# Cross-attention scores paired on the two row halves of TensorE, with scratch laid out for 4 KB reads

## What is computed

```python
# x, ctx: 8 x 256 x 512, float32; 32 query heads of 16 in 8 groups, each group with one key and value head
def layer(x):
    x = x + tanh(g_xattn) * xattn(layernorm(x), ctx, ctx)
    x = x + tanh(g_ffn) * ffn(layernorm(x))
def xattn(q, k, v):
    qh = (q @ Wq.T) -> (8, 32, 256, 16);  kh, vh = (k @ Wk.T), (v @ Wv.T) -> (8, 8, 256, 16), each repeated 4 times
    attn = softmax(qh @ kh.T / sqrt(16))
    return (attn @ vh) @ Wfc.T + bfc
def ffn(h):
    comb = sum(softmax(top_2(h @ router.T)))
    return mlp(h, shared 2048) + mlp(h, routed 256) * comb      # mlp: silu(h @ g.T) * (h @ u.T) @ d.T
```

## Time and profile before

| | us |
|---|---|
| Three runs: median (lowest, highest) | 951.03 (944.7, 956.66) |
| The profiled execution | 942.72 |
| Its span, first to last instruction | 940.9 |
| TensorE busy, granted clock over the span | 899.5, 0.987 of full speed |
| VectorE, ScalarE, GpSimd busy | 646.6, 343.4, 486.7 |

### The profile page before, as it was taken

The page is one execution under the profiler, slowest core; times in us unless marked ns, Lnnn a source line. Parts: engine busy times, 40 slices in busy tenths (PEclk is TensorE's granted clock), DMA queues, the critical chain, the costliest instruction groups (busy, mean ns, idle before and its releaser), DMA issues.

```text
span 940.9 us, 14873 instructions
## 1 busy us (share of the span) xinstructions
PE 899.5 (96%) x4896; PEld 697.8 (74%) x4896; DVE 646.6 (69%) x1083; ACT 343.4 (37%) x637; POOL 486.7 (52%) x485
## 2 busy tenths in 40 slices
PE   4689999999999999999999999999999999999998
PEld 3556766676677665688888888887688888888887
DVE  6678888778878887566656566567766656566566
ACT  5165566556655686212212122136212211122112
POOL 4201201300130299878766696663778766696650
PEclk9789999999999999999999999999999999999999
DMA  8863344435343420211111121111312111121102
GB/s 277 201 144 80 78 116 74 108 80 118 62 96 83 87 37 25 90 45 67 45 60 52 45 67 45 45 57 56 112 45 68 45 54 57 45 67 45 45 1 89
DMA packets 42346, 70.83 MB, mean 75 GB/s; under 512 B 5312, under 2 KB 21184, under 8 KB 42048
## 3 DMA queue, kind: packets, MB, share of 16 engines
q1 hardware_dynamic: 42304, 70.29, 27.9%
HBM read 55.33 MB, written 14.68 MB: 74 GB/s over the span
## 4 chain that ended last, share of the span: by engine, by line
PE 72%; issue 17%; DVE 4%; DMA 3%; POOL 2%; ACT 2%; SPq 0%; POOLq 0%; DVEq 0%; ACTq 0%
PE bank L1241 21%; PE bank L1243 20%; PE bank L1242 20%; PE bank L1316 3%; PE bank L1296 3%; PE bank L1306 3%; PE bank L1246 1%; POOL xa L461 1%; DMA q_scr<-qx_l 1%; POOL cx_l L430 1%; DVE mcol L887 1%; PE bank L1565 1%; DVE x_l L1206 1%; DMA wfc_raw<-wfc 1%; DMA xa<-x 1%
## 5 line engine op out<-in xcount | busy, mean ns | idle before, releaser
L887 DVE TENSOR_REDUCE mcol<-bank 128x2 f32<-128x512 f32 x256 | 169.8, 677 | 48.9 <-PE bank L1296 48.1
L1241 PE MATMUL bank<-x_l,w_h 128*128 128x512 f32 x504 | 197.5, 392 | 2.7 <-DVE u L1077 2.5
L1243 PE MATMUL bank<-x_h,w_h 128*128 128x512 f32 x504 | 196.4, 390 | 0.0
L1242 PE MATMUL bank<-x_h,w_l 128*128 128x512 f32 x504 | 196.4, 390 | 0.0
L740 ACT ACTIVATE probs<-bank 128x512 f32<-128x512 f32 x256 | 150.1, 594 | 120.6 <-PE bank L1306 119.5
L595 ACT ACTIVATE hT_h<-bank 128x512 fp32r<-128x512 f32 x72 | 43.2, 599 | 360.3 <-DVE bank L1179 351.5
L551 POOL TENSOR_TENSOR w_l<-raw,w_h 128x512 fp32r<-128x512 f32 (+1 forms) x144 | 162.1, 1159 | 2.9
L1089 DVE SCALAR_TENSOR_TENSOR xa<-bank,tgf,xa 128x512 f32<-128x512 f32 x128 | 96.1, 751 | 77.7 <-PE bank L1243 77.6
L1296 PE MATMUL bank<-k_st,q_st 65*128 65x256 f32 x512 | 114.0, 312 | 11.8 <-DMA q_st<-q_scr 7.1
L1296 PEld LDWEIGHTS bank<-k_st,q_st 65*128 65x128 f32 x512 | 92.9, 201 | 43.1 <-DVE mcol L887 16.6
L430 POOL TENSOR_TENSOR cx_l<-cx_raw,cx_h 128x512 fp32r<-128x512 f32 x12 | 15.5, 1295 | 191.4 <-ACT cx_h L595 191.4
(11 more groups left out here) (148 smaller groups left out, 1362.8 us busy)
## 6 DMA issues: line engine op xcount, KB each, us to landing
raw<-w_gu SPq DMA_DIRECT2D x36, 512.0 KB, 3.3
q_st<-q_scr SPq DMA_DIRECT2D x96, 128.0 KB, 3.8
dnraw<-w_dn SPq DMA_DIRECT2D x36, 256.0 KB, 2.6
xa<-x SPq DMA_DIRECT2D x4, 1024.0 KB, 7.6
cx_raw<-ctxT SPq DMA_DIRECT2D x16, 256.0 KB, 3.4
q_scr<-qx_h SPq DMA_DIRECT2D x16, 256.0 KB, 2.1
q_scr<-qx_l SPq DMA_DIRECT2D x16, 256.0 KB, 2.2
out<-xa SPq DMA_DIRECT2D x16, 256.0 KB, 2.0
```

The lines of the kernel that those rows point to most:

```text
L887: v.tensor_reduce(mcol[:, par, at:at + 2], bank[u % sm_banks(n)][:, :].rearrange("p (r k) -> p r k", r=2), AX.X, ALU.max).then_inc(max_ok, 1)
L1241: mm(out, a_h, b_l, start=start, stop=False, skip_group_check=onto)
L1242: mm(out, a_l, b_h, start=False, stop=False, skip_group_check=onto)
L1243: return mm(out, a_h, b_h, start=False, stop=stop, skip_group_check=onto)
```

## The change

Queries, keys and matmuls are arranged anew for two groups of heads at once.

- **Row halves.** The first group of a chunk has rows 0 to 47, the second rows 64 to 111 (`ROWS` = 64, `SM` = 48 rows for maximum scores, row 48 of each half for the maxima, `ST` = 49). `sm_pair` and `st_pair` issue the two groups' matmuls in turn, on tiles of 64 x 128 of the array, each into a bank of its own. The zero rows are gone, and the memset that made them.
- **Banks.** Maximum scores go round banks 0, 1 and 5. The transposed maxima move from bank 5 to bank 4 (shared with the values, so `mt_job` waits for `ob_ok`, and the value matmuls wait for `mt_cp`). TensorE's order is written by pairs `v` = 0 to 3, with the side work at new places: key and value projections in steps 2 and 3, queries in steps 4 to 7, the output projection of batch 0 in steps 6 and 7.
- **Scratch.** `q_scr` and `k_scr` have the batch outside, and the weights' rows are reordered on the host so that a dimension's four heads lie together: 4 KB a row. A read of queries is now four DMAs, for each half one of 32 rows (source: 2 parts x 16 rows) and one of 16 rows; so is a read of keys. A write has two pieces of 1 KB a row.
- **SyncE.** A `q_st` slot is free when the step's value matmuls are done (`pv_ok`, by `scored`), not its scores (`st_full`). `write_q` of chunk 0, 1, 2 now stands at the end of steps 4, 5, 6 (before: 3, 5 and 6, 6), context loads ahead of `put_max`.
- **Split results** have one place per batch (`aT_h0`, `aT_h1`, and the low parts), `aT` has two; the last batch needs no detour by `qx_h`.

```diff
-CONSTS = 2
-SM = P // 2 + 1
+CONSTS = 1
+SM = 3 * DH
 MROW = SM
 ST = MROW + 1
+ROWS = P // 2
...
-    q_scr = nc.dram_tensor("q_scr", (2, BLOCKS, CHUNKS, P, BLOCK), f32, kind="Internal").ap()
-    k_scr = nc.dram_tensor("k_scr", (2, BLOCKS, P, BLOCK), f32, kind="Internal").ap()
+    q_scr = nc.dram_tensor("q_scr", (2, BLOCKS, CHUNKS, 2, P, S), f32, kind="Internal").ap()
+    k_scr = nc.dram_tensor("k_scr", (2, BLOCKS, 2, P, S), f32, kind="Internal").ap()
...
+        def sm_bank(n, s, u):
+
+            return bank[u % 4] if isinstance(n, int) and n < 2 else bank[(0, 1, 5)[(UNITS * s + u) % 3]]
...
+            def scored(n):
+
+                sp.wait_ge(pv_ok, 4 * n)
...
-                for row, part in ((0, 0), (DH, 0), (2 * DH, 1)):
-                    src = q_scr[part, tb, c, :, bb * S:(bb + 1) * S].rearrange("(h d) q -> d h q", d=DH)
-                    sp.dma_start(r(q_st[row:row + DH, c, :, :]), src).then_inc(q_rd[c], 16)
+            def write_q(tb, oc):
+                for part, (done, tile) in enumerate(((q_hi, qx_h), (q_lo, qx_l))):
+                    sp.wait_ge(done, CHUNKS * tb + oc + 1)
+                    sp.dma_start(q_scr[part, tb, oc, :, :, :].rearrange("b p q -> p b q"),
+                                 r(tile[:, oc % 2, :]).rearrange("p (b q) -> p b q", q=S)).then_inc(q_wr[oc], 16)
...
+            def read_q(tb, bb, c, n, fresh):
+
+                if not fresh:
+                    scored(n)
+                sp.wait_ge(q_wr[c], 32 * (tb + 1))
+                for e in range(2):
+                    at, rows = e * ROWS, slice(e * ROWS, (e + 1) * ROWS)
+                    sp.dma_start(r(q_st[at:at + 2 * DH, c, :, :]).rearrange("p h q -> p (h q)"),
+                                 q_scr[0:2, tb, c, bb, rows, :].rearrange("a (d h) q -> a d (h q)", d=DH)).then_inc(q_rd[c], 16)
+                    sp.dma_start(r(q_st[at + 2 * DH:at + 3 * DH, c, :, :]).rearrange("d h q -> d (h q)"),
+                                 q_scr[0, tb, c, bb, rows, :].rearrange("(d h) q -> d (h q)", d=DH)).then_inc(q_rd[c], 16)
...
+                for e in range(2):
+                    at, rows = e * ROWS, slice(e * ROWS, (e + 1) * ROWS)
+                    sp.dma_start(r(k_st[at:at + DH, bb, :, :]).rearrange("d c q -> d (c q)"),
+                                 k_scr[0, tb, bb, rows, :].rearrange("(d c) q -> d (c q)", d=DH)).then_inc(k_rd[bb], 16)
+                    sp.dma_start(r(k_st[at + DH:at + 3 * DH, bb, :, :]).rearrange("p c q -> p (c q)"),
+                                 k_scr[0:2, tb, bb, rows, :].rearrange("a (d c) q -> a d (c q)", d=DH)).then_inc(k_rd[bb], 16)
...
+                    if s == 4 and not last:
+                        read_k(t + 1, 0)
+                    if s >= 4 and not last:
+                        write_q(t + 1, s - 4)
...
-                        if not last and s in (3, 6) and u == 0:
-                            q_low(nx, s // 6)
...
+                        if (s, u) in ((4, 7), (5, 5), (6, 5), (7, 5)):
                             q_low(nx, s - 4)
...
+                    pe.wait_ge(max_ok, UNITS * n + 2 * v - (0 if s == 0 and v == 0 else 1))
                 for j in range(2):
...
+                    for e in range(2):
+                        rows = slice(e * ROWS, e * ROWS + SM)
+                        last = mm(sm_bank(n, s, 2 * v + e)[:, j * S:(j + 1) * S],
+                                  q_st[rows, c, 2 * half + j, qt * P:(qt + 1) * P], k_st[rows, bb, c, :],
+                                  start=True, stop=True)
+                        if j == 1:
+                            last.then_inc(sm_full[e], 1)
...
+                    pe.wait_ge(exp_ok, UNITS * n + 2 * v)
+                for e in range(2):
+                    rows = slice(e * ROWS, e * ROWS + ST)
+                    mm(STB[e][:, :], k_st[rows, bb, c, kt * P:(kt + 1) * P], q_st[rows, c, 2 * half:2 * half + 2, :],
+                       start=True, stop=True).then_inc(st_full[e], 1)
```

More of the change, by code:

```diff
@@ L108, in build @@
         att.close()
-        def a_split(high, last_batch):
-            if last_batch:
-                part = qx_h if high else qx_l
-                return part[:, :, :].rearrange("p a (b q) -> p (a b) q", q=S)
-            return aT_h if high else aT_l
+        a_split = {True: (aT_h0, aT_h1), False: (aT_l0, aT_l1)}
         pflat = probs[:, :, :, :].rearrange("p a r s -> p (a r s)")
@@ L338, in body @@
                     n = STEPS * t + s
-                    if s + 3 < STEPS or not last and s != 6:
+                    if s + 3 < STEPS or not last:
                         e = s + 3
@@ L541, in split_gu @@
             def split_gu(G, f):
-                if isinstance(G, int) and G < 2:
-                    pool.wait_ge(st_full, UNITS * (N - 2) if G == 0 else UNITS * N)
-                else:
+                if is_at(G, 1):
+                    pool.wait_ge(st_full[0], UNITS // 2 * N)
+                    pool.wait_ge(st_full[1], UNITS // 2 * N)
+                if not (isinstance(G, int) and G < 2):
                     pool.wait_ge(full[3], G - 1)
@@ new lines, in body @@
+                        if not first:
+                            if s in (1, 2) and u == 3:
+                                f_sum(t - 1, 1, s - 1)
+                            if s == 1 and u == 7:
+                                f_stats(t - 1, 0, 1)
+                            if s == 2 and u == 6:
+                                f_stats(t - 1, 1, 0)
+                            if s == 3 and u == 4:
+                                f_stats(t - 1, 1, 1)
+                        if last:
+                            if (s, u) in ((5, 3), (6, 1)):
+                                f_sum(t, 0, s - 5)
+                            if (s, u) in ((6, 4), (7, 4)):
+                                f_stats(t, 0, s - 6)
+                            if s == 0 and u == 0:
+                                dve.wait_ge(ln2_stats, HTILES)
+                                for i in range(HTILES):
+                                    aggregate(1, i, ln2_var)
+                            if s == 0 and u == 5:
+                                norm2_rows(0, 0, HTILES)
+                            continue
@@ L1286, in f_part @@
                     last.then_inc(f_mm, 1)
-            def sm_unit(n, u, bb, c):
-                qt, g2, half = u // 2 % 2, u // 4, u % 2
-                banks = sm_banks(n)
-                if not (isinstance(n, int) and n == 0 and u < banks):
-                    pe.wait_ge(max_ok, UNITS * n + u + 1 - banks)
-                for j in range(2):
-                    h = g2 * RH + half * 2 + j
-                    last = mm(bank[u % banks][:, j * S:(j + 1) * S], q_st[0:SM, c, h, qt * P:(qt + 1) * P],
-                              k_st[0:SM, bb, 2 * c + g2, :], start=True, stop=True)
-                last.then_inc(sm_full, 1)
@@ new lines, in st_pair @@
+            def st_pair(n, v, bb, c):
+                kt, half = v // 2, v % 2
+                if isinstance(n, int) and n == 0 and v == 0:
+                    pe.wait_ge(max_ok, 2 * UNITS)
+                else:
+                    pe.wait_ge(exp_ok, UNITS * n + 2 * v)
+                for e in range(2):
+                    rows = slice(e * ROWS, e * ROWS + ST)
+                    mm(STB[e][:, :], k_st[rows, bb, c, kt * P:(kt + 1) * P], q_st[rows, c, 2 * half:2 * half + 2, :],
+                       start=True, stop=True).then_inc(st_full[e], 1)
@@ L1476, in body @@
-                        if s == 7 and u == 5 and not last:
-                            pe.wait_ge(q_lo, CHUNKS * nx + 3)
+                                pe.wait_ge(f_add, TILES * t - 2)
+                            x_job(nx, 0)
+                        if s == 0 and v == 3:
+                            pe.wait_ge(x_lo, TILES * nx + 1)
+                            x_job(nx, 1)
+                        if s == 1 and v in (1, 3):
+                            pe.wait_ge(x_lo, TILES * nx + 2 + v // 2)
+                            x_job(nx, 2 + v // 2)
@@ new lines, in body @@
+                        if s == 2 and v == 0:
+                            pe.wait_ge(x_lo, TILES * nx + 4)
+                            vt_job(t, 1)
+                        if s == 2 and v == 1:
+                            pe.wait_ge(vt_cp, 2 * t + 2)
+                            kv_part(nx, 0, 0)
+                        if s == 2 and v == 2:
+                            if not first:
+                                pe.wait_ge(f_add, TILES * t)
+                            kv_part(nx, 1, 0)
```

527 lines of the change are left out of this document (251 added, 276 removed).

## The result

| | before | after |
|---|---|---|
| Median, us (lowest, highest) | 953.85 (944.7, 958.81), 4 runs | 1032.17 (1024.39, 1037.6), 4 runs |
| Ratio, 95% interval | | 1.0827 (1.0714 to 1.0939) |
| Profiled execution, us | 942.72 | 1037.6 |

The forecast was 980 us with a range up to 998: the direction was right, the size was not. On the profiled execution's scale it was 972 against 1037.6, 66 us too low.

A forecast was written before the change was run, and what follows sets the result against it. TensorE bounded the kernel before, VectorE close behind; after, late reads on two engines would. Three blocks 22, last block 3 and start 4.6 add 29.6 us to 942.7: 972, 980 on the median's scale; range 912 to 998, the forecast's own 962 to 998.

The forecast's parts named there:

- The two engines: Query and key reads: each 32-row DMA with a 2-part source runs on two DMA engines, inferred from small-packet counts.
- The step as a chain of read, scores, values, next issue: Attention step: the next read is issued after the values and its landing gates the next scores; at least 9.85 us.
- Step 5's write behind the key read: Step 5's query read needs a write queued behind the key read: 7 us more a block.
- The pairs' 1.88 us: Attention scores on TensorE: two paired matmuls cost one, saving 1.88 us a step at best.
- the 0.5 for cuts: TensorE in attention: five more changes of the array's cut add 0.5 us a step.
- The feed-forward part: After attention: every matmul there is unchanged, so it should stay at 550 us.
- rival (a): Attention: reads on all 16 engines, pairs overlap, steps of 9.5 us; 31 us less, 920; chance 0.30.
- Rival (c): Attention: reads on 16 engines, pairs run one after another, cut changes add 16 us, 967; chance 0.08.
- 4.6 more: Kernel start: slower first reads delay the first transposed scores from 51.23 to 55.8 us.
- 3 x 92.0 = 276: First three attention blocks: each takes 92.0 us against 84.8, 7.2 more, 22 in all.
- 136 / 16 x 0.7 = 5.95 us, landed 7.85 us after the first issue.: A step's reads on two engines: 5.95 us of transfer plus 1.9 fixed, against 3.8 us landing before.
- 2.0 us into the step.: When a step's read is issued: after 0.5 us of score pairs, 1.0 of values, 0.5 for end and wake-up.

The follow-up runs named there:

- e1_wide: Changed kernel with only its read patterns re-cut to an outermost count of 16, for sixteen DMA engines: 914.23 us, ratio 0.9606 to the kernel before.
- e2_scored: Changed kernel, reads left on two engines; SyncE waits ahead of a read for the previous step's transposed scores, not its values: 989.38 us, ratio 1.0402.
- e3_order: Changed kernel, reads left on two engines; in step 4 the first query chunk's write goes ahead of the key read: 1014.32 us, ratio 1.0645.
- e4_same: e1_wide with both groups' score matmuls on the first group's rows, so a pair shares one row half: 971.22 us, ratio 1.0209 to the kernel before.
- e11_again: The changed kernel itself, unaltered, measured again beside e10_rows on the same chip: 1026.54 us, ratio 1.0758 to the kernel before.
- e10_rows: Changed kernel with unused 128-row matmuls ahead of the waits of steps 1 (10) and 6 (26), except the first block's step 1: 1020.53 us, ratio 1.0683.
- e9_fill: Changed kernel with unused 48-row matmuls ahead of the long waits, 10 in step 1 and 26 in step 6: 1025.53 us, ratio 1.0757.

## Why the prediction failed in size

**Right.** The two engines, from the census. The step as a chain of read, scores, values, next issue: e1_wide breaks it at the landing, e2_scored at the issue, and both shorten it. Step 5's write behind the key read (e3_order). The pairs' 1.88 us, and roughly the 0.5 for cuts (e4_same: 1.88, and 0.2 to 0.4). In the 1.88 there was luck: the value matmuls are on column strips, not on row halves, and they stand twice as dense as the maximum scores (1.00 / 16 = 0.06 us against 0.12), not four times as I had read. The feed-forward part. And rival (a), "the reads run on all 16 engines and the pairs overlap", 31 us less: e1_wide made it true, and its profiled execution is 29.1 us under that of before (942.72 - 913.62), with steps of 9.35 us where I had 9.5 (by the medians it is 39 us, 914 against 953). Rival (c), 967, is e4_same's 971.

**Wrong.** By the same cuts, the 66 us that I missed lie in three places. The second key read of the first block went out at 76.87 us instead of 57.76, 19.1 later where the forecast had "4.6 more": 14.5. The three blocks took 318.2 us where the forecast had 3 x 92.0 = 276: 42.2. And from 395.03 us to the end it is 640.7 us against 628.7 from 312.18, 12 more where the forecast had 3: 9. The steps that failed:

- *"136 / 16 x 0.7 = 5.95 us, landed 7.85 us after the first issue."* Reads with nothing ahead of them landed after 8.6 to 8.8 us (141.61 to 150.22 and 243.65 to 252.49 in e11_again, 251.95 to 260.65 in after). The 0.7 us came from two medians whose difference is small, so an error of 15% was hidden in it: 136 KB / (8.7 - 1.9) us is 20 KB a us, not 22.9. The plain steps bear it out: 2.0 + 8.7 = 10.7, and from the read of step 6 to those of step 7 and of the next step 0 it is 10.8 and 10.7 (263.80, 274.57, 285.24). That is 0.85 us in each of 24 steps of the three blocks, 20 us.
- *"2.0 us into the step."* The 0.5 for pairs and 1.0 for values hold at full clock only. After the 7.5 us wait the next read went out 3.1 us behind the first score. That a wait lowers the clock of the work behind it had no term in my sum at all, and this is the error of kind, not of size. TensorE's busy time is 85.4 us a block against 73.0 in e1_wide with the same instructions, 12 us of stretched work; of it e10_rows shows 1.7 us on the path behind one of the waits. With 20 us for the landing, 22 of the blocks' 42 are left, 7 a block, for the clock behind all waits and for what I have not found. By SyncE's read issues 12.7 of them lie in steps 0 to 2, which share their engines with context loads and a key read (43.1, 40.2 and 40.1 us, where 3 x 10.7 + 2.8 + 2.0 = 36.9 would be the forecast with the landing put right), and 6.9 in steps 4 and 5 (31.6, 32.2 and 32.5 against 29.8), of which e10_rows takes 4.0 off. How much of the 12.7 is clock and how much queueing no run tells.
- *"27.25 + 1.9 + 4 x 5.95 + 2.8 = 55.8: 4.6 more"*, the start. The first transposed scores, to which this figure is compared, began at 65.49 us, 14.3 after those of before (51.23), and the first steps add the other 4.8 of the 19.1. In e1_wide the second key read goes out at 62.45, 4.7 later than before, though its first scores wait for their read for 4.9 us only (6.0 before); the two engines add 14.4. I had counted the transfers but not SyncE's own waits. The second query read could not be issued until its write, itself queued behind the first key read, had landed: 34.94 to 40.05 in the timeline of SyncE. The third chunk's write stands behind it in SyncE's order and went out at 42.31 (37.82 in e1_wide), and the first scores wait 13.0 us.

The range failed for the same reason. Its upper end, 998, took in a key read that hides nowhere, not a mechanism by which one lateness makes the next: read late, clock low, next issue later.

## What to carry to other kernels

Read the access pattern of a DMA from its outermost dimension: here a source with 2 outermost was carried by two engines, though its rows were 4 KB, and putting the dimension of 16 outside took a step's reads from 8.7 to 4.6 us and the kernel from 1032 to 914. Making scratch rows longer does not make up for it. When a transfer turns from hidden to late, count everything that follows: who issues the next one, behind which work, and at what clock that work runs after a wait.

## What the hardware showed that I had not expected

- What two engines cost the others' transfers. Context loads on 16 engines took 7.5 us while the reads ran on two of them, 3.4 in the kernel before, and 2.8 once the reads were spread (e1_wide), with the same bytes in all.
- TensorE's granted clock fell from 1.00 to 0.50 inside a run of back-to-back matmuls of 48 rows (e9_fill, at 252 us), and stayed at 1.00 through as many of 128 rows (e10_rows, 243.85 to 249.9) and through 1.66 us of wait behind them. It did so in all three blocks of each run. The two fills also differ in cut and values, so the rows are not shown to be the reason.
- Two matmuls on rows 0 to 47 and 64 to 111, each into its own bank, cost as much as one: 0.66 us for six (e1_wide) that take 1.13 in one row half (e4_same).
